# Layer 0 of a two-layer transformer block: normalisations written with one tensor and two scalars, and both 8-bit roundings on ScalarE

## What is computed

```python
def act_quant(x, bits):
    qb = float(2 ** (bits - 1) - 1)
    scale = qb / jnp.clip(jnp.max(jnp.abs(x), axis=-1, keepdims=True), EPS, None)
    q = jnp.clip(jnp.round(x * scale), -qb, qb) / scale
    return _ste(x, q)
def hbitlinear(x, w, bits):
    xq = act_quant(fwht(x), bits)
    wq = weight_quant(w)
    return jnp.einsum('bsd,fd->bsf', xq, wq)
h = hbitlinear(hidden_states, w_up, ACT_BITS)
h = jnp.square(jax.nn.relu(h))
return hbitlinear(h, w_down, ACT_BITS)
...
x = x + jnp.tanh(g_xattn[0]) * _L0_xattn_ref(_layernorm(x, axis=-1), ...)
x = x + jnp.tanh(g_ffn[0]) * _L0_ffn_ref(_layernorm(x, axis=-1), ...)
```

## Time and profile before

| | |
|---|---|
| time, median of 3 | 1274.38 us (1273.2 to 1280.59) |
| profiled execution, its own time | 1277.01 us |
| span of the profiled execution | 1275.2 us |
| mean granted clock of TensorE | 0.963 |
| busy of the span: TensorE, VectorE, ScalarE, GpSimd | 88%, 83%, 72%, 58% |

### The profile page before, as it was taken

The page is one execution under the profiler, slowest core; times in us unless marked ns, Lnnn a source line. Parts: engine busy times, 40 slices in busy tenths (PEclk is TensorE's granted clock), DMA queues, the critical chain, the costliest instruction groups (busy, mean ns, idle before and its releaser), DMA issues. The chain is left out here.

```text
span 1275.2 us, 30386 instructions
## 1 busy us (share of the span) xinstructions
PE 1127.3 (88%) x8831; PEld 909.0 (71%) x8831; DVE 1059.4 (83%) x2484; ACT 917.7 (72%) x3601; POOL 738.8 (58%) x1084
## 2 busy tenths in 40 slices
PE   3688888877899999999999999999899999659992
PEld 2345555544588888888888888888787788549981
DVE  5779999997788888988998888888689887756664
ACT  4556666656999899899989989989788888313330
POOL 5357777766766656655666665665455888323331
PEclk9689999998999999999999999999999999969996
DMA  7454544442140202202211220220321100533326
GB/s 177 77 80 84 80 73 74 79 72 49 41 135 2 88 2 88 87 12 75 87 46 41 87 85 2 87 87 0 125 67 55 35 35 35 223 117 90 96 68 202
DMA packets 135320, 97.05 MB, mean 76 GB/s; under 512 B 59069, under 2 KB 128830, under 8 KB 135232
## 3 DMA queue, kind: packets, MB, share of 16 engines
q1 hardware_dynamic: 125680, 84.18, 26.0%
q0 software_dynamic: 3408, 8.45, 1.8%
q10 hardware_dynamic: 6144, 3.35, 0.9%
HBM read 55.02 MB, written 41.56 MB: 76 GB/s over the span
## 5 line engine op out<-in xcount | busy, mean ns | idle before, releaser
L1550 POOL TENSOR_TENSOR head_rstd<-head_rstd,minus_half 128x4 f32<-128x4 f32 x192 | 225.7, 1176 | 15.1
L1538 ACT ACTIVATE squares<-ps 128x128 bf16<-128x128 f32 x768 | 201.8, 284 | 42.8 <-PE ps L1501 35.0
L1501 PE MATMUL ps<-w_proj_in,xq 128*128 128x512 f16 (+1 forms) x1024 | 209.5, 327 | 5.9 <-ACT headsT L1574 5.3
L1630 POOL TENSOR_TENSOR prob<-prob,rinv 128x512 f32<-128x512 f32 x128 | 140.4, 1097 | 107.9 <-DVE rinv L1625 107.7
L1574 ACT ACTIVATE headsT<-ps,l_hln 128x256 f32<-128x256 f32 (+1 forms) x256 | 167.9, 689 | 30.2 <-PE ps L1565 30.2
L1617 ACT ACTIVATE prob<-ps,nmax 128x128 f32<-128x128 f32 x512 | 182.2, 390 | 9.6 <-DVE nmax L1608 8.1
L1538 ACT ACTIVATION_READ_ACCUMULATOR squares<-ps 128x1 f32 x768 | 165.3, 216 | 0.0
L1558 DVE TENSOR_TENSOR heads_n<-ps,head_rstd 128x512 f32<-128x512 f32 x192 | 131.1, 683 | 25.9 <-POOL head_rstd L1550 25.6
L1501 PEld LDWEIGHTS ps<-w_proj_in,xq 128*128 (+1 forms) x1024 | 100.0, 98 | 53.1 <-issue 8.5
L1601 PE MATMUL ps<-headsT 128*128 128x128 f32 x1024 | 136.2, 276 | 1.0 <-DVE probT L1646 0.4
L1601 PEld LDWEIGHTS ps<-headsT 128*128 128x128 f32 x1024 | 128.3, 192 | 8.0 <-issue 5.4
(11 more groups left out here) (321 smaller groups left out, 2601.3 us busy)
## 6 DMA issues: line engine op xcount, KB each, us to landing
slots<-blank_slot SPq DMA_DIRECT2D x12, 1554.0 KB, 7.7
halves<-half_made SPq DMA_DIRECT2D x32, 256.0 KB, 2.5
w_proj_in<-halves SPq DMA_DIRECT2D x16, 512.0 KB, 9.1
w_out_raw<-in_wprojT SPq DMA_DIRECT2D x8, 512.0 KB, 3.8
half_raw<-in_winT SPq DMA_DIRECT2D x16, 256.0 KB, 2.9
half_raw<-in_woutT SPq DMA_DIRECT2D x16, 256.0 KB, 3.0
taken<-slots SPq DMA_DIRECT2D x15, 259.0 KB, 3.3
q_rows<-q_parts SPq DMA_DIRECT2D x48, 64.0 KB
```

What stands on the lines that cost most here:

```text
L1501: last = e.matmul(out, xq[:, k, which, slot_at], weights(k, hl, c0, n), start=(k == 0 and hl == 0), stop=(k == KD - 1 and hl == 1))
L1538: last = e.activation(squares[:, 4 * n + h, :], A[n][:, h * HD1:(h + 1) * HD1], ACT.Square, scale=HD1**-0.5, accum_out=hss[:, 4 * n + h:4 ...
L1550: e.tensor_tensor(hr[:, four], hr[:, four], t["half"][:, four], ALU.pow).then_inc(g_r[n].sem, 1)
L1630: e.tensor_tensor(prob[:, kind, :, :], prob[:, kind, :, :], spread(rinv[:, kind, :], P), ALU.mult).then_inc(g_p[kind].sem, 1)
```

## The change

The two normalisations (P2 and F2) become one operation with a tensor and two per-partition scalars; before they read a second tensor, rstd spread over the columns. Of the two quantisations VectorE keeps the maximum and the step; the roundings become pieces F3r and F6r on ScalarE, which scales and adds MAGIC in one instruction and subtracts it in the next, with a wait between them. The step of F6q has one operation less, for which the scale of the up weights gets a factor FF^-0.25 once. F4v and F7s on GpSimd now wait for the step only. Where TensorE waited for v_q1 or v_q2 it waits for both counts of a_g1 or a_g2.

```diff
-        "EX:5 P2a+++ F2a- EX:6 EX:7 P3h+++ OC:1 EX:0+ EX:1+ F4a- EX:2+ F4s- OTa WH++ F7a-- EX:3+ NTh++ EX:4+ "
+        "EX:5 P2a+++ F2a- EX:6 F6r-- EX:7 P3h+++ OC:1 EX:0+ F3r- EX:1+ F4a- EX:2+ F4s- OTa WH++ F7a-- EX:3+ NTh++ EX:4+ "
...
+        chain.link(e.tensor_scalar(w_step[:, 0:1], w_step[:, 0:1], FF**-0.25, None, ALU.mult))
...
-        e.scalar_tensor_tensor(xn[:, :], row(i), mv[:, 0:1], rstd[:, 0:1].to_broadcast([P, D]),
-                               ALU.subtract, ALU.mult).then_inc(p_xn.sem, 1)
+        e.tensor_scalar(xn[:, :], row(i), mv[:, 0:1], rstd[:, 0:1], ALU.subtract, ALU.mult).then_inc(p_xn.sem, 1)
...
-        e.scalar_tensor_tensor(yn[:, :], row(i), mv_f[:, 0:1], rstd_f[:, 0:1].to_broadcast([P, D]),
-                               ALU.subtract, ALU.mult).then_inc(f_yn.sem, 1)
+        e.tensor_scalar(yn[:, :], row(i), mv_f[:, 0:1], rstd_f[:, 0:1], ALU.subtract, ALU.mult).then_inc(f_yn.sem, 1)
...
     def _(e, i, p):
         e.wait_ge(g_sum.sem, g_sum.at(i))
-        e.wait_ge(v_q2.sem, v_q2.at(i - 1))
+        e.wait_ge(a_g2.sem, a_g2.at(i - 1))
...
-    def quantise(e, chain, quant, src, norm, c, rnd, out, done):
+    def step_of(e, chain, quant, src, norm, c):
         chain.link(e.tensor_reduce(quant[:, c:c + 1], src, AX, ALU.max, apply_absolute_value=True))
-        if c == 4:
-            chain.link(e.tensor_tensor(quant[:, c:c + 1], quant[:, c:c + 1], quant[:, 7:8], ALU.mult))
         chain.link(e.tensor_scalar(quant[:, c:c + 1], quant[:, c:c + 1], norm, EPS, ALU.mult, ALU.max))
         chain.link(e.reciprocal(quant[:, c + 1:c + 2], quant[:, c:c + 1]))
-        if c == 4:
-            chain.link(e.tensor_scalar(quant[:, c + 2:c + 3], quant[:, c + 1:c + 2], quant[:, 7:8], 127.0 * norm,
-                                       ALU.mult, ALU.mult))
-        else:
-            chain.link(e.tensor_scalar(quant[:, c + 2:c + 3], quant[:, c + 1:c + 2], 127.0 * norm, None, ALU.mult))
-        chain.link(e.tensor_scalar(rnd, src, quant[:, c + 2:c + 3], MAGIC, ALU.mult, ALU.add))
-        e.tensor_scalar(out, rnd, MAGIC, None, ALU.subtract).then_inc(done.sem, 1)
...
+        chain.last(e.tensor_scalar(quant[:, c + 2:c + 3], quant[:, c + 1:c + 2], norm, 127.0, ALU.mult, ALU.mult))
...
+    @s.piece("F3r", "scalar")
+    def _(e, i, p):
+        e.wait_ge(c_f3.sem, c_f3.at(i))
+        e.activation(rnd1[:, :], F1[:, 0:D], ACT.Copy, bias=MAGIC, scale=quant[:, p, 2:3]).then_inc(a_g1.sem, 1)
+        e.wait_ge(a_g1.sem, a_g1.at(i, 1))
         e.wait_ge(pe_q1.sem, pe_q1.at(i - 1))
...
+        e.activation(q1[:, :], rnd1[:, :], ACT.Copy, bias=-MAGIC).then_inc(a_g1.sem, 1)
...
+    @s.piece("F6r", "scalar")
+    def _(e, i, p):
+        e.wait_ge(c_f6.sem, c_f6.at(i))
+        e.activation(rnd2[:, :], F1[:, :], ACT.Copy, bias=MAGIC, scale=quant[:, p, 6:7]).then_inc(a_g2.sem, 1)
+        e.wait_ge(a_g2.sem, a_g2.at(i, 1))
         e.wait_ge(pe_q2.sem, pe_q2.at(i - 1))
...
+        e.activation(q2[:, :], rnd2[:, :], ACT.Copy, bias=-MAGIC).then_inc(a_g2.sem, 1)
```

More of the change, by code:

```diff
@@ L65, in link, with last, at @@
         self.engine.wait_ge(self.sem, self.i * self.per + self.n)
+    def last(self, instruction):
+        instruction.then_inc(self.sem, 1)
+        self.n += 1
+    def at(self, i):
+        return i * self.per + self.per
     def end(self):
@@ L676, in layer0 @@
     pe_yT, a_yT, pe_h1 = sig("pe_yT", "tensor"), sig("a_yT", "scalar"), sig("pe_h1", "tensor")
-    v_q1, g_two, pe_q1, a_q1 = sig("v_q1", "vector"), sig("g_two", "gpsimd", 2), sig("pe_q1", "tensor"), sig("a_q1", "scalar")
+    a_g1, g_two, pe_q1, a_q1 = sig("a_g1", "scalar", 2), sig("g_two", "gpsimd", 2), sig("pe_q1", "tensor"), sig("a_q1", "scalar")
     pe_up, a_hid = sig("pe_up", "tensor"), sig("a_hid", "scalar", 2)
     g_sum, g_fly, g_scale = sig("g_sum", "gpsimd"), sig("g_fly", "gpsimd", 2), sig("g_scale", "gpsimd")
-    pe_h2, v_q2 = sig("pe_h2", "tensor"), sig("v_q2", "vector")
+    pe_h2, a_g2 = sig("pe_h2", "tensor"), sig("a_g2", "scalar", 2)
     pe_q2, a_q2, pe_dn, v_x2 = sig("pe_q2", "tensor"), sig("a_q2", "scalar"), sig("pe_dn", "tensor"), sig("v_x2", "vector")
@@ L1036, in _ @@
         e.wait_ge(pe_h1.sem, pe_h1.at(i))
+        step_of(e, c_f3, quant[:, p, :], F1[:, 0:D], D**-0.5, 0)
+        c_f3.end()
+    @s.piece("F3r", "scalar")
[3 more added lines that the diff above has]
+        e.wait_ge(a_g1.sem, a_g1.at(i, 1))
         e.wait_ge(pe_q1.sem, pe_q1.at(i - 1))
-        quantise(e, c_f3, quant[:, p, :], F1[:, 0:D], D**-0.5, 0, rnd1[:, :], q1[:, :], v_q1)
-        c_f3.end()
+        e.activation(q1[:, :], rnd1[:, :], ACT.Copy, bias=-MAGIC).then_inc(a_g1.sem, 1)
     @s.piece("F4v", "gpsimd")
     def _(e, i, p):
-        e.wait_ge(v_q1.sem, v_q1.at(i))
+        e.wait_ge(c_f3.sem, c_f3.at(i))
         e.tensor_tensor(quant[:, p, 3:4], quant[:, p, 0:1], w_step[:, 0:1], ALU.mult).then_inc(g_two.sem, 1)
@@ L1049, in _ @@
     def _(e, i, p):
-        e.wait_ge(v_q1.sem, v_q1.at(i))
+        e.wait_ge(a_g1.sem, a_g1.at(i))
         e.wait_ge(a_yT.sem, a_yT.at(i))
@@ L1065, in _ @@
         e.wait_ge(a_q1.sem, a_q1.at(i))
-        e.wait_ge(v_q1.sem, v_q1.at(i))
-        filling(e, i, (v_q2, -1), (v_x2, -2), (a_q2, -2))
+        e.wait_ge(a_g1.sem, a_g1.at(i))
+        filling(e, i, (a_g2, -1), (v_x2, -2), (a_q2, -2))
         for m in range(KF):
@@ L1095, in _ @@
         e.wait_ge(v_x2.sem, v_x2.at(i - 1))
-        filling(e, i, (a_q2, -1), (a_hid, 0), (v_q1, 0))
+        filling(e, i, (a_q2, -1), (a_hid, 0), (a_g1, 0))
         for k in range(KF):
@@ L1105, in _ @@
         e.wait_ge(g_two.sem, g_two.at(i))
+        step_of(e, c_f6, quant[:, p, :], F1[:, :], quant[:, p, 7:8], 4)
+        c_f6.end()
+    @s.piece("F6r", "scalar")
[3 more added lines that the diff above has]
+        e.wait_ge(a_g2.sem, a_g2.at(i, 1))
         e.wait_ge(pe_q2.sem, pe_q2.at(i - 1))
-        quantise(e, c_f6, quant[:, p, :], F1[:, :], FF**-0.5, 4, rnd2[:, :], q2[:, :], v_q2)
-        c_f6.end()
+        e.activation(q2[:, :], rnd2[:, :], ACT.Copy, bias=-MAGIC).then_inc(a_g2.sem, 1)
     @s.piece("F7", "tensor")
     def _(e, i, p):
-        e.wait_ge(v_q2.sem, v_q2.at(i))
+        e.wait_ge(a_g2.sem, a_g2.at(i))
         if not isinstance(i, int) or i + 1 < B:
             e.wait_ge(a_hid.sem, a_hid.at(i + 1))
-        filling(e, i, (v_q1, 1), (v_q2, 0), (v_x2, -1))
+        filling(e, i, (a_g1, 1), (a_g2, 0), (v_x2, -1))
         for k in range(KF):
@@ L1130, in _ @@
         e.wait_ge(a_q2.sem, a_q2.at(i))
-        filling(e, i, (a_hid, 1), (v_q1, 1), (v_q2, 0))
+        filling(e, i, (a_hid, 1), (a_g1, 1), (a_g2, 0))
         for k in range(KF):
@@ L2204 @@
     ),
-    "scalar": (
-        "aaaaaaaaaaaaaaaaaaaaaaaaaaaaaaaaabbbaaaabaaabaaabaabaabbaabcaaaabaabababaababccbbbacbbbbabababbbccbb"
-        "babbbbbbbbbbcbbbbbbbbcbbbbbb"
-    ),
+    "scalar": "aaaaaaaaaaaaaaaaaaaaaaaaaaaaaaaaaaaaabbbaaaabaaaabaaaabaabaabbaabcaaaabaaabaababaababccbbbaaacbbbbababaabbbccbbbabbbbbbbbbbcbbbbbbbbcbbbbbb",
     "gpsimd": "aaaaaaaaaaabaaaaaaaaaabaaaaaaabbaababababaababaabbbabbabbbbbbbbbbbbbbbbbbbbbbbb",
```

4 lines of the change are left out of this document (2 added, 2 removed).

## The result

The changed kernel takes 1289.7 us (median of 4 runs, 1288.34 to 1291.14) against 1275.59 us for the kernel before in the same job (4 runs, 1273.2 to 1280.59). The ratio is 1.0109, with a 95% interval from 1.0089 to 1.0129: slower by 1.1%. The prediction had 1282 us and called "within 1%" the likeliest; the time lies inside its range (1255 to 1292), but the case that came was rival C, which had a chance of 0.20. The profiled execution took 1289.85 us, with a span of 1288.1.

The account below looks back on a forecast made before the run. The loop was taken as bound by a ring through GpSimd's WL, yn and F3, not VectorE's 95%; ten rounds +5 us and the mixed part +3 us gave +8, 1282 us, range 1255 to 1292.

Parts of the forecast that it names:

- rival C: Mixed part, 285 to 345 us: ScalarE becomes the limit, its fixed order holding layer 1 behind roundings; 1291 us, chance 0.20.
- The ring: Loop round of 17.04 us: yn on VectorE ends only when GpSimd's WL ends; some 1.8 us of VectorE's time is standing.
- Rival A: VectorE's queue is the limit after all, so removing the roundings wins 1.2 us a batch: 1255 us, chance 0.16.
- rival B: The one-tensor yn is not held beside WL and ends some 1.87 us earlier: 1270 us, chance 0.07.
- The normalisations: yn and xn in the new form: yn still ends with WL but 0.13 us nearer, xn 0.07 us shorter.
- From yn to F3: Loop, F6q and F6r: with roundings on ScalarE this way takes 2.95 us instead of 2.73, costing 0.2 us.
- From F3 to XB: Loop, F3q and F3r: ScalarE's roundings delay F4u, S:4 and xn, so XB starts at +8.05 instead of +7.58.
- the prediction's own sum: Loop round from F3 to F3: 8.05 + 6.45 + 0.15 + 2.95 = 17.6 us against 17.04.
- In the mixed part ... I take 0.6 to 0.8 us each: +3 us: End of layer 0 with start of layer 1: four batches add 2.2 us each to ScalarE, mostly fitting its gaps.
- The even rounds: Loop of layer 0, 110 to 285 us: ten rounds, each taken as 0.5 us longer, +5 us.
- a rounding that waits over 0.5 us at ScalarE's head: Mixed part: the sign named for ScalarE's fixed order holding layer 1's squares and exponentials.
- the stretch behind 285 us grows by over 6 us: Mixed part: growth named as showing the forecast wrong and ScalarE the limit there.

Follow-up runs that it names:

- The exchange of WL: In GpSimd's list WL goes behind F3b instead of ahead of it; done alone on the kernel before 1276.2 us, on the changed kernel 1277.0 us.
- wl_late_before: The kernel before with only WL put behind F3b in GpSimd's list: 1276.2 us, ratio to before 0.9996.
- wl_late_mixed: Changed kernel with WL behind F3b on GpSimd and the mixed part's roundings back on VectorE: 1263.8 us, ratio to before 0.9886.
- last_two_on_vector: The changed kernel with the four roundings of batch elements 14 and 15 given back to VectorE: 1279.4 us, ratio to before 1.0027.
- mixed_on_vector: The changed kernel with the mixed part's roundings (F3q from element 11, F6q from 10) back on VectorE: 1277.1 us, ratio to before 0.9997.

## Why the prediction was wrong

**The ring: right.** yn ends with WL in every kernel that has WL ahead of F3b, and taking 20 us from VectorE in 175 us changed the round by 0.1 us. Rival A (0.16) and rival B (0.07) fell with it. B fell by yn itself, 2.04 us beside WL. The exchange of WL shows the ring by another way: with yn free the next instruction of the same kind is caught and the round stays (17.2 to 17.3), and with that one out of the way too it is 15.9.

**The normalisations: right in kind, 0.13 + 0.07 us predicted, 0.21 to 0.22 measured.** yn ends 0.15 us behind WL instead of 0.28, and xn takes 0.40 instead of 0.48 (means of nine rounds). The page GPSIMD Engine Reference of the Trainium skill, section Specifications, speaks of contention with VectorE's two-input and two-port instructions. The runs here agree: yn is held with two inputs and with one, and so is q2 (one input, 2.23 us instead of 0.43). No run shows which port mode an instruction is in.

**From yn to F3: right.** 2.95 us predicted, 2.87 measured, against 2.78 before (mean of nine rounds). ScalarE's chain with its shorter step costs 0.09 us there, where the prediction had 0.2. Its round of 17.04 us was one of the shorter ones: they alternate between about 17.05 and 17.3, with a mean of 17.2.

**From F3 to XB: the step that failed in the rounds.** Predicted +8.05 instead of +7.58; measured, as a mean of nine rounds, +7.60 against +7.70. F4u came 0.68 us later, not 0.87, and S:4 followed it by 0.89 us, not 1.15 (before: 1.33), so that S:4 was only 0.24 us late. Before, the score products had waited more for VectorE to read the maxima of earlier ones; now VectorE waits for the products as well. The waits from 110 to 285 us, before and then after:

```profile
PEld ps L844 <- DVE nmax L852: 12.9, 31, 4.0
...
DVE nmax L852 <- PE ps L844: 1.0, 1, 1.0
```

```profile
PEld ps L851 <- DVE nmax L859: 7.5, 13, 4.0
...
DVE nmax L859 <- PE ps L851: 7.3, 21, 1.4
```

In the 3.6 us ahead of xn VectorE had no idle time before (172.35 to 176.00), and has 0.54 and 0.17 us in two waits for products now. So P2 was late in the kernel before because VectorE's list had no gap ahead of it, not because of S:4, and the 0.8 us of rounding that left this list made room for what TensorE lost. Besides, GpSimd itself ends L1051 at about +7.4, so that XB waited for xn 4 times in 16, by 1.5 us in all, where the prediction had 0.4 us each time. With +7.60 in place of +8.05 the prediction's own sum gives 17.15 us a round; the mean of nine rounds is 17.11.

**"In the mixed part ... I take 0.6 to 0.8 us each: +3 us": the step that decided the result.** It measured +11.8 us. The even rounds gave -1.1 us instead of +5. The sum treated added work as something that a busy engine absorbs in proportion to its free time. Rival C had the mechanism, its price (+10) and its sign (a rounding that waits over 0.5 us at ScalarE's head: it was 1.85 and 4.17), and "the stretch behind 285 us grows by over 6 us" was named as what would make the forecast wrong. But C was priced by 2.2 us for each of four or five elements, and it is the four pairs of instructions of the last two that make 10 of the 14 us. The order of the program and the timeline of the kernel before had it to be read: behind the last F6r, ScalarE's list has squares, rowsT_n and two pieces of w_proj_out of layer 1, and the trace of before has them at 352.4 to 356.4 us, ahead of the time at which F6q of element 15 gave its step (357.7). C's total of 1291 was right by luck, as it rested on +5 from the rounds, which did not come, and on 2.2 us for too many elements.

The page ScalarE: Activation LUTs of the Trainium skill, section Rules for kernel authors, tells to keep add and mul on VectorE, since VectorE is faster per element. For q2 alone the trace agrees, 0.43 us on VectorE and 0.63 on ScalarE; rnd2, which reads PSUM, takes 0.75 and 0.69. The time of the whole kernel does not follow from that here: the same two roundings on ScalarE cost 0.23 us a round in the loop, 10 us at two elements in the mixed part, and the loop's are worth 1.1% once WL stands where it would hold VectorE's version (ratio 0.9996 in wl_late_before, 0.9886 in wl_late_mixed; the new normalisations, which lie between them too, are worth nothing alone).

**What stays open.** last_two_on_vector leaves 4 us to mixed_on_vector that I can't give to single instructions, and of the 14 us the part that TensorE's lower clock adds is not separated (last section).

## What to carry to other kernels

Before moving work to an engine with a fixed order, look at each place where it will stand and ask what is queued behind it and when its input comes: in the even loop here the added work cost 0.23 us a round, and at the seam between two stages a rounding that came before its input held everything behind it. When an instruction of VectorE is stretched beside GpSimd, look at what will lie beside GpSimd's long operation once it is moved: here the exchange alone only picked the next victim, and it paid when that instruction ran on another engine. The exchange alone (0.9996) and the roundings moved in the loop alone (0.9997, mixed_on_vector) were worth nothing, and together 1.1%.
